# Token rows kept in token order in DRAM and gathered tile by tile; the norm's scale and shift folded into W1 and b1

## What is computed

```python
out = jnp.einsum('btc,ec->bte', soma * gate, Wout)
out = (out - mu) / jnp.sqrt(var + 1e-05) * gamma + beta        # 'z' below
...
logits = x @ Wr + br                     # x is the normalised row here
idx = jnp.argmax(logits, axis=-1)
gates = ...                              # softmax probability of idx
for ei in range(8):
    h = jax.nn.gelu(xf @ W1[ei] + b1[ei], approximate=False)   # 128 -> 512
    y = h @ W2[ei] + b2[ei]                                    # 512 -> 128
    out = out + y * (gf * (idxf == ei))[:, None]
```

## Time and profile before

| | us |
|---|---|
| median of three runs | 229.62 |
| lowest and highest | 228.37, 230.73 |
| the profiled execution | 228.22 |
| its span in the trace | 226.5 |

### The profile page before, as it was taken

How to read it: one execution, slowest core, us unless ns; L and a number is a source line. 1 busy time by engine, 2 the same in 40 slices (tenths; PEclk the granted TensorE clock), 3 DMA queues, 4 the chain that set the end, 5 groups by cost and what they waited for, 6 DMA issues and landing times.

```text
span 226.5 us, 4763 instructions
## 1 busy us (share of the span) xinstructions
PE 176.7 (78%) x1677; PEld 132.3 (58%) x1677; DVE 115.2 (51%) x353; ACT 115.0 (51%) x268; POOL 63.3 (28%) x93
## 2 busy tenths in 40 slices
PE   2769689999997969995999959999720009999990
PEld 1327467776654534653568537999620008999980
DVE  6466685479855420530161479796475003555530
ACT  3756633886778555861463816422490003556540
POOL 8998002005200040000020020000674720355442
PEclk9979955799999788996799988999955555999996
DMA  4456355290003510250000399000000338000000
GB/s 118 123 129 191 73 177 153 53 335 6 9 1 85 174 35 0 87 170 26 3 0 3 103 367 269 4 3 0 3 0 23 117 114 283 26 16 26 26 10 0
DMA packets 21085, 18.91 MB, mean 84 GB/s; under 512 B 4029, under 2 KB 18608, under 8 KB 21062
## 3 DMA queue, kind: packets, MB, share of 16 engines
q1 hardware_dynamic: 19606, 16.86, 24.9%
q0 software_dynamic: 896, 1.59, 2.1%
q10 hardware_dynamic: 560, 0.16, 0.3%
HBM read 8.54 MB, written 4.03 MB: 55 GB/s over the span
## 4 chain that ended last, share of the span: by engine, by line
PE 59%; DVE 12%; DMA 8%; SPq 7%; issue 5%; POOL 4%; ACT 4%; DVEq 0%; POOLq 0%
PE ps L1018 7%; SPq L394 6%; PE ps L1031 6%; PE ps L891 6%; PE ps L611 5%; PE ps L848 5%; DMA t_Ks<-t_parts 4%; PE ps L828 4%; PE ps L677 4%; PE ps L814 3%; PE ps L606 3%; POOL z_dram L589 3%; DVE t_mx L1413 3%; PE ps L817 3%; PE ps L714 2%
## 5 line engine op out<-in xcount | busy, mean ns | idle before, releaser
L1325 ACT ACTIVATE t_v_pad<-ps,t_b_tile 128x128 f32<-128x128 f32 x60 | 17.2, 368 | 32.2 <-PE ps L1018 32.2
L1168 ACT ACTIVATE t_P<-ps 128x512 f32<-128x512 f32 x32 | 19.1, 603 | 18.4 <-PE ps L817 18.2
L1413 DVE TENSOR_REDUCE t_mx<-ps 128x4 f32<-128x512 f32 x32 | 21.8, 688 | 10.8 <-PE ps L677 10.3
L1136 ACT ACTIVATE t_P<-ps 128x512 f32<-128x512 f32 x32 | 18.8, 601 | 8.3 <-PE ps L700 3.9
L559 POOL TENSOR_SCALAR t_rstd<-t_mv 128x4 f32<-128x4 f32 (+2 forms) x5 | 1.4, 279 | 75.0 <-DVE t_mv L1482 75.0
L594 POOL DMA_INDIRECT out_dram<-t_v_pad,t_Qs x15 | 15.1, 1006 | 25.1 <-DVE t_v_pad L1684 24.4
L1018 PE MATMUL ps<-t_zsT,t_late 128*128 128x128 f32 x120 | 17.8, 297 | 0.2 <-DVE t_zsT L1680 0.2
L1010 PE MATMUL ps<-t_ident,t_Qs 128*128 128x128 f32 x15 | 4.3, 304 | 16.9 <-DMA t_Qs<-z_dram 16.9
L814 PE MATMUL ps<-t_bandb,t_identb 128*128 128x512 bf16 x32 | 13.5, 421 | 4.9 <-DMA t_Ks<-t_parts 4.9
L1542 DVE SCALAR_TENSOR_TENSOR t_Qs<-t_v_pad,t_mod,t_blend 128x128 f32<-128x128 f32 x64 | 17.1, 347 | 0.1
L1031 PE MATMUL ps<-t_Ks,t_v_pad 128*128 x120 | 16.9, 284 | 0.0
(11 more groups left out here) (265 smaller groups left out, 361.9 us busy)
## 6 DMA issues: line engine op xcount, KB each, us to landing
t_Qs<-t_parts SPq DMA_DIRECT2D x24, 128.0 KB
t_Ks<-t_parts SPq DMA_DIRECT2D x24, 128.0 KB
t_Ks<-in_L_ffn_W_dram SPq DMA_DIRECT2D x1, 2048.0 KB, 9.5
z_dram<-t_empty_row SPq DMA_DIRECT2D x1, 1935.0 KB, 8.5
t_Qs<-z_dram SPq DMA_DIRECT2D x1, 1032.0 KB, 6.9
t_Qs<-z_dram SPq DMA_DIRECT2D x1, 645.0 KB, 4.2
t_rows<-in_fside_BxSxS_dram SPq DMA_DIRECT2D x2, 256.0 KB, 3.2
t_x_tok<-in_x_dram SPq DMA_DIRECT2D x2, 256.0 KB, 3.7
```

The costliest lines, as they stand in the source:

```text
L1136: act.activation(P[:, u % 3, :], SCORE_BANKS[u % 2][:, :], ACT.Exp, scale=SCALE).then_inc(scores_read, 1)
L1168: act.activation(P[:, (UNITS + u) % 3, :], ps[u % 4][:, :], ACT.Sigmoid, scale=SCALE).then_inc(window_scores_read, 1)
L1325: m = act.activation(hsT[:, n % 2, cs], ps[n % 2][:, cs], ACT.Gelu, bias=b1_tile[:, n % 2, c:c + 1])
L1413: dve.tensor_reduce(mx[:, b, 4 * g:4 * g + 4], MAX_BANKS[u % 2][:, :].rearrange("p (j t) -> p j t", j=4), AX.X, ALU.max).then_inc(max_scor ...
```

## The change

The table in DRAM now has 1,024 rows in token order and one empty row. A row is x1, z, gate: 257 values. SP stores x1 as soon as each half is ready, and z with the gate once `gate_ready` is given; for that VectorE computes the gate before it waits for the rank. The scatter and the reload are gone. In their place VectorE derives from the slots a one-hot matrix of each token's place within its tile and the tile it lies in, and TensorE multiplies the two (sixteen bf16 products) into `perm`: for each slot of each tile the token in it. GpSimd gathers each tile by `perm` (`fetch`), six tiles ahead, then one fetch behind each output scatter.

The norm's gamma and beta are no longer applied to z. gamma scales W1's rows as W1 is copied for a tile (the copy of line 1677 becomes a multiply by a per-partition scalar). beta times W1 is added to b1: `fold_beta` has 32 products of a 128x128 block of W1 with one column, half of them ahead of the rank products, half behind. The results lie in a new job `b1` on a PSUM bank of the alternating list, and `perm` is the next job on that bank. Two broadcast loads of gamma and beta go.

```diff
         x_tok = sb("x_tok", [128, NB, D])
 
-        ROW = 2 * D + 2
-        GATE, TOKEN = 2 * D, 2 * D + 1
+        ROW = 2 * D + 1
+        GATE = 2 * D
         rows = sb("rows", [128, NB, ROW])
-        z, x1 = rows[:, :, 0:D], rows[:, :, D:2 * D]
...
-        ZS_CUTS = (0, 2, 7, TILES)
-        zs_part = lambda i: sum(i >= c for c in ZS_CUTS[1:])
+        AHEAD = 6
...
         alternating += ["mod_0", "x1T_1", "ctxT_1", "h1_1", "gate_1", "mod_1",
-                        "tg_0", "o_0", "tg_1", "o_1", "tg_2", "oT_0", "o_2", "oT_1", "lg_0", "lg_1", "rank"]
+                        "tg_0", "o_0", "tg_1", "o_1", "tg_2", "oT_0", "o_2", "oT_1", "lg_0", "lg_1", "b1", "rank", "perm"]
...
             sp.wait_ge(tile_zero, 1)
-            sp.dma_start(z_dram.rearrange("(i p) c -> p i c", p=128), bc_mid(empty_row[:], TILES)).then_inc(z_zeroed, 16)
+            sp.dma_start(z_dram[NT:NT + 1, :], empty_row[:]).then_inc(z_zeroed, 16)
...
-            sp.wait_ge(z_out, 16 * NB)
-            for k in range(3):
-                a, z_ = ZS_CUTS[k], ZS_CUTS[k + 1]
-                sp.dma_start(zs[:, a:z_, :], z_dram[a * 128:z_ * 128].rearrange("(i p) c -> p i c", p=128))\
-                    .then_inc(zs_in[k], 16)
+            token_rows = z_dram[0:NT].rearrange("(b s) c -> s b c", b=NB)
+            for half in range(2):
+                bs = slice(half * HALF, half * HALF + HALF)
+                sp.wait_ge(x1_ready, half + 1)
+                sp.dma_start(token_rows[:, bs, 0:D], x1[:, bs, :]).then_inc(x1_out, 16)
+            sp.wait_ge(z_scaled, 2)
+            sp.wait_ge(gate_ready, 1)
+            for half in range(2):
+                bs = slice(half * HALF, half * HALF + HALF)
+                sp.dma_start(token_rows[:, bs, D:ROW], rows[:, bs, D:ROW]).then_inc(z_out, 16)
...
-            norm_z(0)
-            norm_z(1)
-
-            pool.wait_ge(slot_ready, 1)
-            pool.wait_ge(gate_ready, 1)
-            pool.wait_ge(z_ready, 2)
-            pool.wait_ge(token_no, 1)
+
+            def fetch(i):
+
+                pool.indirect_dma_start(out=zs[:, i, :], out_offset=None, in_=z_dram,
+                                        in_offset=bass.IndirectOffsetOnAxis(perm[:, i:i + 1], 0)).then_inc(zs_in[i], 16)
+
             pool.wait_ge(z_zeroed, 16)
-            for b in range(NB):
-                pool.indirect_dma_start(out=z_dram, out_offset=bass.IndirectOffsetOnAxis(slot[:, b:b + 1], 0),
-                                        in_=rows[:, b, :], in_offset=None).then_inc(z_out, 16)
-
+            pool.wait_ge(x1_out, 32)
+            pool.wait_ge(z_out, 32)
+            job_wait_read(pool, "perm")
+            for i in range(AHEAD):
+                fetch(i)
             for i in range(TILES):
                 pool.wait_ge(y_read, i + 1)
                 pool.indirect_dma_start(
                     out=out.rearrange("b s c -> (b s) c"),
-                    out_offset=bass.IndirectOffsetOnAxis(zs[:, i, TOKEN:TOKEN + 1].bitcast(U32), 0),
+                    out_offset=bass.IndirectOffsetOnAxis(perm[:, i:i + 1], 0),
                     in_=ys[:, i, :], in_offset=None, bounds_check=NT - 1, oob_is_err=False).then_inc(y_out, 16)
+                if i + AHEAD < TILES:
+                    fetch(i + AHEAD)
...
+            def fold_beta(experts):
+
+                for e in experts:
+                    for c in range(FC):
+                        m = pe.matmul(bank_of("b1")[:, e * FC + c:e * FC + c + 1], W1[:, e, c * 128:(c + 1) * 128], gb2[:, 1:2],
+                                      start=True, stop=True)
+                return m
+
+            pe.wait_ge(ld_f, 32)
+            job_wait_free(pe, "b1")
+            fold_beta(range(0, NE // 2))
             pe.wait_ge(onehot_ready, 1)
             pe.wait_ge(rank_consts, 1)
             job_wait_free(pe, "rank")
                 m = pe.matmul(bank[:, W:W + NE], onesb[:], oh[:, W + b * NE:W + (b + 1) * NE], start=(b == 0),
                               stop=(b == NB - 1))
             job_full(m, "rank")
+            job_full(fold_beta(range(NE // 2, NE)), "b1")
+            pe.wait_ge(place_ready, 1)
+            job_wait_free(pe, "perm")
+            for b in range(NB):
+                for k in range(2):
+                    m = pe.matmul(bank_of("perm")[:, 0:TILES], place_hot[:, b, :], token_in[:, b, k, :],
+                                  start=(b == 0 and k == 0), stop=(b == NB - 1 and k == 1))
+            job_full(m, "perm")
 
...
+            job_wait_read(pe, "perm")
             for i in range(TILES + 2):
                 if i < TILES:
-                    pe.wait_ge(zs_in[zs_part(i)], 16)
+                    pe.wait_ge(zs_in[i], 16)
...
-                    pe.transpose(ps[4 + i % 2][:, 0:128], zs[:, i, 0:D], ident[:]).then_inc(zT_full, 1)
+                    pe.transpose(ps[4 + i % 2][:, 0:128], zs[:, i, D:2 * D], ident[:]).then_inc(zT_full, 1)
...
             dve.tensor_tensor(onehot, cand[:], bc_last(emin[:], NE), ALU.is_equal).then_inc(onehot_ready, 1)
+            dve.wait_ge(gexp_ready, 1)
+            link(dve.tensor_reduce(gsum[:], gexp[:], AX.X, ALU.add))
+            dve.reciprocal(rows[:, :, GATE], gsum[:]).then_inc(gate_ready, 1)
             job_wait_full(dve, "rank")
             bank = bank_of("rank")
             W = NB * NE
             link(dve.tensor_tensor(cmp[:], tri8[:], bc_mid(tiles_e[:], NE), ALU.mult))
             link(dve.tensor_reduce(excl[:], cmp[:], AX.X, ALU.add))
 
-            dve.wait_ge(gexp_ready, 1)
-            link(dve.tensor_reduce(gsum[:], gexp[:], AX.X, ALU.add))
-            dve.reciprocal(rows[:, :, GATE], gsum[:]).then_inc(gate_ready, 1)
-
             link_job(dve.scalar_tensor_tensor(cand[:], bc_mid(excl[:], NB), 128.0,
                                               bank[:, 0:W].rearrange("p (b e) -> p b e", e=NE), ALU.mult, ALU.add), "rank")
             link(dve.tensor_tensor(cand[:], cand[:], onehot, ALU.mult))
             link(dve.tensor_reduce(slotf[:], cand[:], AX.X, ALU.add))
-            dve.tensor_copy(slot[:], slotf[:]).then_inc(slot_ready, 1)
+            dve.wait_ge(token_no, 1)
+            link(dve.tensor_tensor(reached[:], bc_last(slotf[:], TILES + 1), bc_mid(tile_starts[:], NB), ALU.is_ge))
+            dve.tensor_tensor(in_tile[:], reached[:, :, 0:TILES], reached[:, :, 1:TILES + 1], ALU.subtract)
+            link(dve.tensor_reduce(tile_f[:], reached[:], AX.X, ALU.add))
+            dve.tensor_scalar(token_in[:, :, 0, :], in_tile[:], token_col[:, 0:1], None, ALU.mult)
+            link(dve.scalar_tensor_tensor(place[:], tile_f[:], -128.0, slotf[:], ALU.mult, ALU.add))
+            dve.tensor_tensor(token_in[:, :, 1, :], in_tile[:], bc_last(batch_base[:], TILES), ALU.mult)
+            dve.tensor_tensor(place_hot[:], bc_last(place[:], 128), bc_mid(places[:], NB), ALU.is_equal)\
+                .then_inc(place_ready, 1)
 
             link(dve.tensor_tensor(incl[:], excl[:], tiles_e[:], ALU.add))
             link(dve.tensor_tensor(tmap_c[:], bc_mid(incl[0:1, :], TILES), bc_last(tile_no[:], NE), ALU.is_le))
             link(dve.tensor_reduce(tmap_f[:], tmap_c[:], AX.X, ALU.add))
             dve.tensor_scalar(tmap[:], tmap_f[:], float(NE - 1), None, ALU.min).then_inc(tmap_ready, 1)
+            job_wait_full(dve, "b1")
+            job_wait_read(dve, "wC2")
+            link_job(dve.tensor_tensor(b1T[:].rearrange("p e c -> p (e c)"), b1T[:].rearrange("p e c -> p (e c)"),
+                                       bank_of("b1")[:, 0:NE * FC], ALU.add), "b1")
+            job_wait_full(dve, "perm")
+            job_read(dve.tensor_scalar(perm[:], bank_of("perm")[:, 0:TILES], float(NT), None, ALU.add), "perm")
...
-            job_wait_read(dve, "wC2")
...
                     dve.tensor_copy(b1_tile[:, i % 2, :], b1T[:, bass.ds(e, 1), :].rearrange("p a f -> p (a f)"))
-                    dve.tensor_copy(W1_tile[:, i % 2, :], W1[:, bass.ds(e, 1), :].rearrange("p a f -> p (a f)"))\
+                    dve.tensor_scalar(W1_tile[:, i % 2, :], W1[:, bass.ds(e, 1), :].rearrange("p a f -> p (a f)"),
+                                      gb2[:, 0:1], None, ALU.mult)\
                         .then_inc(w1_ready, 1)
                     dve.wait_ge(zT_full, i + 1)
                     dve.tensor_copy(zsT[:, i % 2, :], ps[4 + i % 2][:, 0:128]).then_inc(zT_read, 1)
...
                     dve.scalar_tensor_tensor(ys[:, n, :], ps[6 + n % 2][:, 0:D], zs[:, n, GATE:GATE + 1],
-                                             zs[:, n, D:2 * D], ALU.mult, ALU.add).then_inc(y_read, 1)
+                                             zs[:, n, 0:D], ALU.mult, ALU.add).then_inc(y_read, 1)
```

## The result

| | before | after |
|---|---|---|
| median of 20 runs each | 229.27 us (224.49 to 240.3) | 232.84 us (229.03 to 240.95) |
| profiled execution | 228.22 us, span 226.5 | 232.50 us, span 230.8 |
| start of the last router products | 163.15 | 163.87 |
| first transpose of the expert loop | 187.00 | 184.46 |
| from there to the start of the first result | 6.06 | 6.77 |

The change costs time: the ratio after to before is 1.021, 95% interval 1.013 to 1.029, where 230.0 us had been predicted and no measurable change was the likeliest case.

A forecast was written before the change was run, and what follows sets the result against it. The prediction took a routing hole in TensorE's work, then TensorE's pace over 15 tiles, as the bound. Start -3.3 and loop +3.7 gave +0.4 us on the 229.62 median: 230.0, range 226.3 to 235.3 (forecast's own 228.7 to 232.0).

The forecast's parts named there:

- no measurable change: Whole kernel: the forecast 230.0 us with its small errors, nearly all within about 1% (227.3 to 231.9); chance 0.46.
- rival (a): Expert loop: the register move before each scatter does not hide, pair 3.07 us, 235.3 us; chance 0.25 with a dear gather.
- Rival (b): Expert loop: the clock falls while TensorE idles 0.57 of each 2.57 us, giving 232 to 234 us; chance 0.10.
- The first fold: Ahead of the rank products: 32 instructions at 0.215 us, 6.9 in all, rank products read at 172.8.
- Rival (c): Both folds before the first fetch run warm, about 3.8 us each instead of 6.9, giving 225.8 us; chance 0.08.
- The one-hot: Routing: without GpSimd's passes the one-hot is ready some 2 us earlier, at 167.3, a gain not collected.
- The place products: After the second fold and b1's addition: products start at 179.8, take 0.7 us, first fetch at 181.0.
- The fetch's landing: Ahead of the first and last tile: 2.6 us from issue to landing, with ends 2.3 and 3.2.
- The pair: Expert loop: one scatter and one fetch occupy GpSimd 2.57 us against TensorE's 2.0 a tile; TensorE waits 3.7.
- the dear gather: Expert loop: a gather takes GpSimd 1.2 us instead of 0.96, adding 1.9; chance 0.25 together with rival (a).
- Rival (d): Expert loop: GpSimd keeps up, a pair at 2.1 us or less, giving 226.3 us; chance 0.08.
- W1's multiply: Expert loop, VectorE: gamma in W1's copy adds up to 0.32 us a tile, hidden by 0.4 of slack.

The follow-up runs named there:

- e3: Changed kernel with both halves of the beta-times-W1 fold behind the rank products, output the same; median 240.34 us against 229.59 for the kernel before.
- e4: Changed kernel with the fold's products 128 columns wide (identity in place of the beta column), output differs; median 230.12 us against 229.59 before.
- e5: Kernel before, with gamma and beta applied in the copy of the transposed tile out of PSUM, not by GpSimd; median 227.24 us, ratio to before 0.996.
- e11: Changed kernel with empty slots sent to 128 different zero rows instead of one; median 232.31 us against 229.36 for the kernel before.
- e12: Changed kernel with a bounds check so that the fetch leaves out empty slots; median 230.75 us against 229.36 for the kernel before.
- e1: Changed kernel with all 15 fetches ahead of the first output scatter instead of six; median 226.34 us, ratio to before 1.005.
- e7: Kernel of e6 with all 15 fetches ahead of the first output scatter; median 220.02 us against 228.99 before, ratio 0.963.
- e9: Kernel of e7 with 8 fetches ahead in place of 15; median 223.46 us against 228.81 for the kernel before.
- e10: Kernel of e7 with 10 fetches ahead in place of 15; median 221.29 us against 228.81 for the kernel before.
- e8: Changed kernel once more, unedited; median 233.08 us against 228.99 for the kernel before, ratio to before 1.016.
- e6: Changed kernel without the fold, W1 plainly copied, gamma and beta applied in the transposed tile's copy out of PSUM; median 226.76 us, ratio to before 1.002.
- e2: Changed kernel without the fold and its addition to b1, beta times W1 left out, output differs; median 227.21 us, ratio to before 0.995.

## Why the prediction fell short, step by step

The median of 232.84 lies in the stated range of 226.3 to 235.3, but above the forecast's own, 228.7 to 232.0 (its upper terms, a landing of 3.2 twice and a pair of 2.7, add to 232.2). It is covered only by the room kept for rivals (a) and (b), and neither of them happened, so that the range held is in part luck. The favoured case, no measurable change (0.46), did not come; slower had 0.37, for reasons that are not the ones below.

The forecast in the terms of the first table, against what came:

| term | forecast | measured | difference |
|---|---|---|---|
| first transpose | 183.7 | 184.46 | +0.8 |
| to the first result's start | 6.06 | 6.77 | +0.7 |
| first to last result | 31.4 | 33.26 | +1.9 |
| last result to end | 5.71 | 6.28 | +0.6 |
| span | 226.9 | 230.77 | +3.9 |

**The first fold: right in price and place.** Forecast were 0.215 an instruction and 6.9 us. The second fold took 6.97 (0.218 an instruction). The first took 6.05, because its first 1.0 us passed at the full clock, which the sum did not count. (The router products end at 165.28 by the earlier trace rows; the sum took 165.1.) Rank read at 172.42 (172.8 forecast). e3 and e4 show both halves of the reason: the price is that of the low clock, and narrow products leave it there. Rival (c) is out.

**The one-hot: right.** Three operations at 0.23, ready at 167.75 (167.3 forecast, with the router 0.7 later here), and the gain was not collected, as said: VectorE waits 2.62 us. e5 collects it. One reading was wrong without effect on the sum: line 1646 did not stand after the passes but beside the fourth, and took 0.22 even so; it reads only one operand from SBUF (e5).

**The place products: right in the sum.** Forecast 179.8, measured 179.58. The last term was too small: from VectorE's conversion to the fetch's start 1.11 us pass (180.26 to 181.37) and not 0.5, with 0.85 of it between the conversion's end and the fetch on a GpSimd that waits for nothing the trace shows (0.28 before), a cause that stays open; the second fold, 0.4 early, and the products, 0.1 shorter, made up for part of it. First fetch 181.37 against 181.0, in an execution whose router came 0.7 later.

**The stores in token order: right.** Issued at 169.87 and 170.27, the second landed at 174.9, over 6 us before the first fetch.

**The fetch's landing: wrong, and the main miss.** I took the scatter of as many rows, 2.6, once ahead of the first tile and once ahead of the last, with 3.2 as the upper end. For full tiles it was nearly right (2.72 to 2.96). But the last fetch belongs to an empty tile, whose 128 slots read the same zero row, and took 3.67: 1.07 of the 1.9 in the loop. The first fetch, of a full tile, took 2.96, which is 0.36 of the 0.8 at the start. What the row of before could not show is that in the scatter no two rows are the same. e11 and e12 show it. The estimate by the Trainium skill (DMA: Bandwidth & Descriptors, Anatomy of one DMA) was 2.3 and lay further off; its fixed part of 2.0 us agrees with the 2.14 of a fetch that moves nothing.

**The pair: right as a mechanism, 3% short.** (214.96 - 193.83) / 8 = 2.64 against 2.57: eight times 0.07 is nearly 0.6. A scatter takes 1.02 in the median and a fetch 0.975, with 0.30 between, which makes 2.60; two pairs took 2.72 and 2.75, where the scatter itself took 1.14 and 1.16. TensorE's recorded waits for fetches in the loop sum to 3.8 us, near the 3.7 of the forecast, but that does not confirm it: the loop lost 5.56, and by the reading given with the busy times part of the waiting stands in the records as busy time. The rest of the 1.9 is 0.15 at the first pair and 0.1 at the end. e1, e7, e9 and e10 show that this term is what made the loop longer.

**The register move: hidden.** The gap ahead of a due scatter is 0.30 with the move in it, so rival (a) is out, and with it the case that I held for the likeliest slower one; the dear gather (1.2 us on GpSimd) too. Rival (b) too: the clock is 1.00 throughout the loop. Rival (d): GpSimd does not keep up, but with more fetches ahead it need not.

**W1's multiply: right.** 

```profile
L1718 DVE TENSOR_SCALAR t_late<-t_Ks,t_gb x15: 485/486/693, 181.5 to 219.2; 128x512 f32 x15
```

0.486 for 128x512 from SBUF, where the copy took 0.426 and the operation out of PSUM 0.75: the double rate of which the Trainium skill (VectorE: DVE Perf Modes, Mode 2x_2P) speaks, and nobody waits for it.

**Two terms that I held for unchanged.** From the first transpose to the first result it took 0.7 longer. The granted clock came back to 1.00 at 190.6, 6.1 us after the first transpose; in the kernel before it did at 192.1, 5.1 after it, and in e5 and e7, where it took 4.9, this stretch is 6.0 and 6.2 us long. So this part varies from run to run with the clock's return; in e8, the changed kernel itself, it took 4.0 and the stretch is 6.1. Over all 14 traces the stretch is 6.0 to 6.3 where the clock came back within 5.1 us of the first transpose, and 6.7 to 7.1 where that took 6.0 us or more. And the end of the span comes 0.57 later after the last result, in every kernel that fetches (6.27 to 6.29) against the two that scatter (5.71 and 5.73). In the records it is GpSimd's drain at the very end, 2.60 us against 2.03, behind 30 indirect DMAs against 23. What it depends on was not tried.

In all, the two large terms had the right sign and the right owner, and what was missed was small and nearly all of one sign: 1.1 from the last landing, 0.7 from the clock's return, 0.6 from the end, 0.6 from the pair, 0.4 from the first landing. As measured the start won 2.5 us (187.00 to 184.46) and not 3.3, and the loop lost 5.6 and not 3.7. "Within 1%" was too narrow a case for a sum in which the two large terms, -3.3 and +3.7, nearly cancel.

## What to carry to other kernels

When a queue has to do a second job for each tile, count the pair against the tile's time, and how many pairs lie between the first result and the last prefetch: here eight prefetches ahead in place of six turned 33.8 us of loop into 28.4 (e6, e9). Put a per-channel scale and shift into a copy that has to be made anyway (0.405 in place of 0.28 us, unseen), rather than into weights, where it took 13 us of TensorE ahead of the critical products and cost some 5 us at the end (e2, e6). And point the padding of a gather at different rows, or leave it out: some 1 us here.

## What the runs showed of the hardware

- A gather of 128 rows of 1,028 bytes lands after 2.7 to 3.0 us if the rows differ (the full tiles of the changed kernel, and all of e11 but one at 3.2) and after 3.6 to 3.7 if all 128 slots read one row; the fewer slots read that row, the less (3.17 for 84, 3.34 for 97). If no row is read at all it is 2.14 (e12).
- TensorE busy without a break for 13.8 us with one-column f32 products had a granted clock of 0.50 all the way (e3); with 128 columns in the same places it came back to 1.00 during the first fold, and 32 instructions of them took 3.82 us against 6.97 (e4).
- An indirect DMA issued from GpSimd occupies it for 0.975 us in the median without a bounds check (fetches of the changed kernel) and 1.02 with one (its scatters; the fetches of e12 1.03), single ones up to 1.2. Between two lie 0.30, also where a register move stands between them: mostly 1.25 to 1.32 per DMA.
- VectorE's 64-column f32 operations of 0.22 us with two SBUF operands took 0.83 to 1.10 beside GpSimd's passes over SBUF, and ended 0.08 after the pass; those with one SBUF operand took 0.22 beside the same passes, and without the passes all took 0.22 to 0.23 (e5).
